# A first routing pass in the lead-out of attention, tables in pieces, and another order of passes and gathers

## What is computed

```
x = x + attention0(layernorm(x)); x = x + swiglu(layernorm(x)); x = x + attention1(layernorm(x))   # causal
z = layernorm(x)
for _ in range(2):                                   # LOOPS
    z_norm = rmsnorm(z) * norm_w
    scores = softmax(z_norm @ router_w)              # 8 experts
    vals, idx = top_k(scores, 2); vals = vals / (sum(vals) + 1e-9)
    mixed = sum over the two chosen e of  vals_e * ((silu(z_norm @ w1[e]) * (z_norm @ w3[e])) @ w2[e])
    z = z + mixed
x = x + z
```

## Time and profile before

| | us |
|---|---|
| median of three runs (2305.61 to 2311.1) | 2308.6 |
| the profiled execution, its own time | 2307.91 |
| its span, first to last instruction | 2306.2 |
| mean granted clock of TensorE | 0.959 of full |
| the attention's last addition to x (L902) ends | 1550.6 |
| first tile's transpose on PE | 1600.0 |
| last issue of the last gather | 2294.4 |

### The profile page before, as it was taken

The page is one execution under the profiler, slowest core; times in us unless marked ns, Lnnn a source line. Parts: engine busy times, 40 slices in busy tenths (PEclk is TensorE's granted clock), DMA queues, the critical chain, the costliest instruction groups (busy, mean ns, idle before and its releaser), DMA issues. The chain is left out here.

```text
span 2306.2 us, 47356 instructions
## 1 busy us (share of the span) xinstructions
PE 2011.8 (87%) x14679; PEld 982.9 (43%) x14679; DVE 1844.3 (80%) x5277; ACT 1462.1 (63%) x3354; POOL 1232.1 (53%) x1710
## 2 busy tenths in 40 slices
PE   5999999999988999899999999974888988988991
PEld 1222222222222465444444444432555766766661
DVE  8999999999999576888888888847777676676555
ACT  1788888888888332677777777751545655655550
POOL 6343343343321021676767676634476777667776
PEclk9999999999999999899999999985999999999996
DMA  7355344344341001434232433302233443433453
GB/s 183 102 130 139 102 130 139 102 129 139 102 129 48 1 19 37 100 70 101 69 99 71 96 74 93 76 26 74 87 106 101 122 117 114 118 108 113 130 139 99
DMA packets 224610, 226.94 MB, mean 98 GB/s; under 512 B 34032, under 2 KB 187504, under 8 KB 224368
## 3 DMA queue, kind: packets, MB, share of 16 engines
q1 hardware_dynamic: 152432, 164.62, 27.0%
q0 software_dynamic: 16384, 33.59, 5.0%
q10 hardware_dynamic: 55552, 25.71, 3.9%
HBM read 96.48 MB, written 125.76 MB: 96 GB/s over the span
## 5 line engine op out<-in xcount | busy, mean ns | idle before, releaser
L702 ACT ACTIVATE mid_PT<-mid_ps 128x512 f32<-128x512 f32 (+2 forms) x1792 | 914.0, 568 | 258.4 <-PE mid_ps L583 250.5
L785 DVE TENSOR_REDUCE mid_nmax<-mid_ps 128x1 f32<-128x512 f32 (+2 forms) x1280 | 776.4, 657 | 61.5 <-PE mid_ps L562 36.4
L562 PE MATMUL mid_ps<-KT,QT 48*128 48x512 bf16 (+3 forms) x2048 | 604.5, 351 | 68.3 <-DVE mid_nmax L785 49.6
L583 PE MATMUL mid_ps<-QT,KT 64*128 64x512 bf16 (+3 forms) x2048 | 562.5, 346 | 2.5 <-ACT mid_PT L702 2.2
L599 PE MATMUL mid_ps<-mid_PT,vv 128*32 128x512 f32 (+3 forms) x4096 | 465.1, 527 | 16.3 <-POOL mid_PT L914 12.5
L562 PEld LDWEIGHTS mid_ps<-KT,QT 48*128 48x128 bf16 x2048 | 158.9, 94 | 585.2 <-DVE mid_nmax L785 397.4
L782 DVE CUSTOM_DVE_ANT_0 mid_PT<-mid_ps,mask 128x512 bf16<-128x512 f32 (+1 forms) x512 | 304.5, 619 | 68.8 <-PE mid_ps L562 64.0
L1395 PE MATMUL moe_ps<-moe_w,moe_xinT 128*128 x638 | 341.5, 618 | 0.0
L1506 POOL DMA_INDIRECT rows_in<-moe_xn,moe_scat_idx x256 | 250.2, 977 | 161.9 <-DVE moe_scat_idx L1696 86.0
L1519 POOL DMA_INDIRECT moe_yg<-rows_out,moe_gat_idx x256 | 250.8, 980 | 80.6 <-issue 77.2
L1450 ACT ACTIVATE moe_xinT<-moe_ps,norm_w 128x128 f32<-128x128 f32 x319 | 116.7, 366 | 275.8 <-PE moe_ps L1407 186.9
(11 more groups left out here) (266 smaller groups left out, 3060.0 us busy)
## 6 DMA issues: line engine op xcount, KB each, us to landing
l_spread<-mid_slots SPq DMA_DIRECT2D x128, 384.0 KB, 5.4
rows_in<-mid_blank SPq DMA_DIRECT2D x64, 512.0 KB, 3.8
QT<-l_spread SPq DMA_DIRECT2D x128, 192.0 KB, 4.3
KT<-l_spread SPq DMA_DIRECT2D x128, 192.0 KB, 5.2
moe_xin<-rows_in SPq DMA_DIRECT2D x319, 64.0 KB
rows_out<-moe_y ACTq DMA_DIRECT2D x319, 64.0 KB
x<-in_L_attn_x_dram SPq DMA_DIRECT2D x8, 512.0 KB, 6.6
QT<-mid_mrows SPq DMA_DIRECT2D x256, 6.0 KB
```

Of the source, the lines that this page charges most:

```text
L562: mm = pe.matmul(ps[:, bank, n_keys * a:n_keys * (a + 1)], QT[rows, par, pair, i * P:(i + 1) * P], KT[rows, par, pair, 0:n_keys], start=Tr ...
L583: mm = pe.matmul(ps[:, bank, m * a:m * (a + 1)], KT[rows, own, pair, i * P:(i + 1) * P], QT[rows, own, pair, SEQ - m:SEQ], start=True, sto ...
L702: act.activation(weights_of(r, i, heads), ps[:, ring(S2, n - 2, k), 0:widths[i] * len(heads)], ACT.Exp, scale=scale).then_inc(exp_done, 1)
L785: dve.tensor_reduce(to, of, X_AXIS, ALU.max, negate=True).then_inc(s1_used, 1)
```

## The change

- Pass 0 moves into the lead-out of the causal attention (new class `Lead`): its norm on DVE to step 64, place 0; the transposes on PE to step 65, places 5 and 7, the router product to place 14; the choice on DVE to step 65, place 15; the count's nine matmuls and the row numbers to the end of step 66, the weights to the end of step 67. POOL issues the first 3 of the 16 DMAs of s0 at the end of step 67, the other 13 at the start of `experts`. Its working space lies in memory that the attention no longer uses.
- SP issues the ten weight loads at the end of the attention's block, after the last weighted values are made (`av_done`). The weights now lie in the buffer of the attention weights.
- Constants of `experts` are made earlier: two by POOL after its first step, others by DVE at step 64. POOL does one `iota` instead of three at the start of `experts`.
- `make_tables` is cut into up to 8 pieces, stages 20 to 27 of a pass, at the spacing of the pass's other stages. Unit 0's pieces run one after another before pass 1. SP waits for a new semaphore, `rows_made`, set by piece 5 (row numbers and experts), and no longer for the last piece.
- `begin` and `transfers` change.

Core of the diff (the body of `Lead` repeats the stages of pass 0 and is cut to its places and waits):

```diff
+class Lead:
+    ZT, SCRATCH, SENT = 14464, 15488, 3
...
+    def tensor(self, pe, off, u, s1_used, s1_total):
+        if (off, u) in ((1, 5), (1, 7)):
+            a = (u - 5) // 2
+            if a == 0:
+                pe.wait_ge(s1_used, s1_total)
+                pe.wait_ge(self.z_ready, 1)
+            for t in range(4):
+                mm = pe.transpose(self.psT[a][:, t * P:(t + 1) * P], self.z[:, 4 * a + t, :], self.w["ident"][:, :])
+            mm.then_inc(self.t_made, 1)
+        if (off, u) == (1, 14):
+            pe.wait_ge(self.t_used, 2)
+            for t in range(IT):
+                mm = pe.matmul(self.psR[:, t, :], self.zT[:, t * P:(t + 1) * P], self.w["router"][:, :], start=True, stop=True)
+            mm.then_inc(self.r_made, 1)
+        if (off, u) == (2, 15):
+            pe.wait_ge(self.const, 2)
+            pe.wait_ge(self.sel_ready, 1)
...
+    def scalar(self, act, off, u):
+        if (off, u) in ((1, 8), (1, 11)):
...
+        if (off, u) == (2, 8):
+            act.wait_ge(self.shifted, 1)
...
+            act.wait_ge(self.second_ready, 1)
...
+    def vector(self, dve, off, u, x_added):
+        if (off, u) == (0, 0):
...
+            dve.tensor_tensor(self.xn[:, :, :], self.z[:, :, :], each_row(rstd), ALU.mult).then_inc(self.xn_ready, 1)
+        if (off, u) == (1, 15):
+            c = self.linked
+            dve.wait_ge(self.r_made, 1)
...
+        if (off, u) == (2, 15):
+            c = self.linked
+            dve.wait_ge(self.k_made, 1)
...
+        if (off, u) == (3, 15):
+            c = self.linked
+            dve.wait_ge(self.exp_ready, 1)
...
+                if lead_pass and n == STEPS + 3:
+                    for i in range(lead_pass.SENT):
+                        lead_pass.scatter(pool, i)
...
             sp.wait_ge(zeroed, 16 * STEPS)
+            sp.wait_ge(second.signals["av_done"], STEPS)
+            load_experts(sp)
...
-    begin = {2: 0, 3: 14, 4: 29, 5: 47, 6: 63, 7: 78, 8: 95, 9: 115, 10: 135, 11: 157, 12: 179, 13: 201, 14: 223, 15: 246,
-             16: 270, 17: 283, 18: 292, 19: 314, 20: 325}
-    transfers = ("s0 s1 s2 s3 g8 s4 s5 g9 s6 g10 s7 g11 s8 g12 s9 g13 s10 g14 s11 s12 g15 s13 g16 s14 g17 g18 s15 "
+    begin = {2: 0, 3: 10, 4: 22, 5: 36, 6: 49, 7: 62, 8: 78, 9: 97, 10: 117, 11: 137, 12: 158, 13: 179, 14: 200, 15: 224,
+             16: 256, 17: 270, 18: 286, 19: 308, 20: 325}
+    transfers = ("s1 s2 s3 g8 s4 s5 s6 g9 s7 g10 s8 g11 s9 g12 s10 g13 s11 g14 s12 g15 s13 g16 s14 g17 s15 g18 "
                  "g19 g20 g21 g22 g23").split()
...
-        return [(k, s) for k, at in begin.items() for s in range(STAGES) if at + s * length(k) // STAGES == n]
+        return [(k, s) for k, at in begin.items() for s in range(STAGES + TABLES) if at + s * length(k) // STAGES == n]
...
-            for k in range(EARLY):
-                for s in range(STAGES):
+            for k in range(1, EARLY):
+                for s in range(STAGES + TABLES):
                     side(k, s)
...
                 if n == base_of[u]:
-                    sp.wait_ge(tables, u + 1)
+                    sp.wait_ge(rows_made, u + 1)
                     for k in range(first_of[u], first_of[u] + sizes[u]):
                         sp.wait_ge(scattered[k % 3], 16 * 2 * IT * (k // 3 + 1))
...
+            for i in range(lead.SENT, 2 * IT):
+                lead.scatter(pool, i)
...
-                    if k + 1 == first_of[unit_of[k]] + sizes[unit_of[k]]:
-                        make_tables(unit_of[k])
+                if s >= STAGES and k + 1 == first_of[unit_of[k]] + sizes[unit_of[k]]:
+                    make_tables(unit_of[k], s - STAGES)
...
+            for part in range(TABLES):
+                make_tables(0, part)
             run(tile, side, 0)
```

More of the change, by code:

```diff
@@ L1073, in middle @@
         after = After(one, ffn.signals)
-        second = attention(nc, ctx, "l1_", ps, shared, x, sides1, kept, center, causal=True, after=after)
+        second = attention(nc, ctx, "l1_", ps, shared, x, sides1, kept, center, causal=True, after=after, lead_pass=lead_pass)
         late = one["late"]
@@ L1180, in experts @@
     BANKS = 3
-    STAGES = 20
+    STAGES, TABLES = 20, 8
     sizes = [1] + [2] * (GROUPS - 1) + [1]
@@ L1705, in make_tables @@
                 full_u, passed_u, shares_u = full[:, :, 0:ht], passed[:, 0:n_tiles, :], shares[:, 0:n_tiles, :]
+                expert, before, live, row = (tab[:, a, 0:n_tiles] for a in range(4))
                 def per(t, n, k=P):
                     return t.unsqueeze(1).to_broadcast([k, n, EXPERTS])
[L1710 to L1712 removed]
@@ L1720, in make_tables @@
-                c.link(dve.tensor_tensor(shares_u, passed_u, per(ntiles[0:1, :], n_tiles, 1), ALU.mult))
-                expert, before, live, row = (tab[:, a, 0:n_tiles] for a in range(4))
-                dve.tensor_reduce(before, shares_u, X_AXIS, ALU.add)
-                c.link(dve.tensor_reduce(expert, passed_u, X_AXIS, ALU.add))
-                c.link(dve.tensor_tensor(before, iota_f[0:1, 0:n_tiles], before, ALU.subtract))
-                dve.tensor_scalar(before, before, float(P), None, ALU.mult)
@@ new lines, in make_tables @@
+                if part == 3:
+                    dve.tensor_reduce(before, shares_u, X_AXIS, ALU.add)
+                    c.link(dve.tensor_reduce(expert, passed_u, X_AXIS, ALU.add))
+                if part == 4:
+                    c.link(dve.tensor_tensor(before, iota_f[0:1, 0:n_tiles], before, ALU.subtract))
+                    dve.tensor_scalar(before, before, float(P), None, ALU.mult)
+                    dve.tensor_scalar(live, expert, EXPERTS - 0.5, None, ALU.is_lt)
+                    c.link(dve.tensor_scalar(row, expert, float(CAP), None, ALU.mult))
+                    c.link(dve.tensor_tensor(row, row, before, ALU.add))
@@ new lines, in make_tables @@
+                if part == 5:
+                    own = slice(base_of[u], base_of[u] + n_tiles)
+                    dve.tensor_tensor(row_of[0:1, own], row, live, ALU.mult)
+                    code = coded[:, :, :].rearrange("o c i -> o (c i)")[:, 0:n_tiles]
+                    c.link(dve.tensor_tensor(code, expert, live, ALU.mult))
+                    c.link(dve.tensor_tensor(weighted[:, 0:n_words, :], coded[:, 0:n_words, :], places[:, 0:n_words, :], ALU.mult))
+                    c.link(dve.tensor_reduce(sums[:, 0:n_words], weighted[:, 0:n_words, :], X_AXIS, ALU.add))
+                    dve.tensor_copy(words[0:1, word_of[u]:word_of[u + 1]], sums[:, 0:n_words]).then_inc(rows_made, 1)
+                    dve.wait_ge(rows_made, u + 1)
```

319 lines of the change are left out of this document (221 added, 98 removed).

## The result

| | median us | runs | lowest to highest |
|---|---|---|---|
| before | 2309.6 | 4 | 2305.6 to 2311.1 |
| changed | 2281.3 | 4 | 2274.6 to 2283.7 |

A forecast was written before the change was run, and what follows sets the result against it. POOL's queue of 31 transfer groups, 20.45 us each, was taken as the bound. Gains of 18.2 + 44.1 = 62.3 from 2307.9 gave 2245.6, with 0.7 for the median 2246; range 2232 to 2271, or 2275 if tiles set the end.

The forecast's parts named there:

- rival of longer issues: POOL's DMA issues: denser DVE work beside them makes each group 1 us longer, 2277 in all; chance 0.05.
- Part 1: Pass 0 moved into the attention's lead-out: 22.7 us removed, 4.5 added, net gain 18.2 us.
- I take 4.5, ends 1 and 8: Attention's end: PE's added transposes, router product and count matmuls delay it by 4.5 us, between 1 and 8.
- between 0 and 1 us: End of the attention's block: SP's ten weight loads end about with it and cost 0 to 1 us, taken as 0.
- DVE part hidden: Lead-out: DVE's first part of pass 0, about 12 us, fits into 15.05 us of idle time and costs nothing.
- Part 2: Expert loop: tables in pieces, earlier passes and a new queue order cut POOL's idle after s1 from 58.1 to 14 us.
- a first-loop pass adds 5.9: Tile times: each first-loop pass adds 5.9 us to its tiles' own 1.63 us each.
- 3.5 per table: Tile times: a table in pieces costs 3.5 us for units 1 to 3, against 7.8 for a whole table.
- I add 4: Row numbers of pass 2: pass 3's stages on DVE, in front of pass 2's last ones, delay them by 4 us.
- gain of 44.1 from pieces, beginnings and queue together: Expert loop: POOL's waits after s1 fall from 58.1 to 14 us, a gain of 44.1, ends 6 and 35.
- third rival: Expert loop: passes begin sooner and end no sooner, POOL's waits remain, only the lead-out's gain counts: 2290; chance 0.03.
- slower rival: Expert loop: 56 table pieces each hold up a tile, then PE runs at half clock; 1.7 us each, 2314; chance 0.02.

The follow-up runs named there:

- e3: Changed kernel with VectorE's z of pass 0 held until POOL's last masks are made: 2279.4 us, 0.9882 of before.
- c1: Changed kernel with only VectorE's first part of pass 0 (statistics, z, xn) in the lead-out, weights loaded in the experts' block; other, slower chip: 0.9942 of before.
- e7: Kernel before with only pass 0 moved into the lead-out; old beginnings, old transfers, whole tables; other, slower chip: 0.9951 of before.
- e1: Changed kernel with the ten weight loads back at the start of the experts' block: 2280.5 us, 0.9889 of before.
- e2: Changed kernel with all sixteen scatters of pass 0 issued in the experts' block, none in the lead-out: 2277.0 us, 0.9873 of before.
- r5: Changed kernel with the beginnings and transfers of before; pass 0 in the lead-out and tables in pieces stay: 2281.4 us, 0.9884 of before.
- r7: Kernel before with only pass 0 moved into the lead-out; old beginnings, old transfers, whole tables: 2300.2 us, 0.9967 of before.

## Why the prediction was wrong

- **What bounds the kernel: right.** POOL's queue of 31 groups, 20.48 us each against 20.45, and a tail of 11.0 against 10.9. The rival of longer issues fell.
- **Part 1, the term "I take 4.5, ends 1 and 8": wrong, 11.3.** The sum of products at the 1.2 GHz level, 6.4, was the upper end, and it is what they cost (2 x 1.11 + 3.58 + 0.56). I let PE's idle time absorb some and priced the attention's own products as before. In fact 1.6 us of idle time were added behind slow masks (2.75 in front of L794 against 1.19 before). The remaining 3.3 are a difference, not a measurement: they fit the attention's own work, which ran at 1.00 from 1536 to 1544 before and at 0.50 until 1552 now. e3 gives the masks 1.5; c1 against e7 gives the products and what goes with them 7.4 of 9.3.
- **Part 1, the block's end at "between 0 and 1 us": wrong, 4.1.** I asked what stands behind the ten loads on SP, and not what the three scatters wait for that share the DMA engines with them. e1 and e2 each remove the gap. "The three early issues gain nothing" was too kind: together with the loads they cost 4. In e2, without them, PE waits 0.95 us for the load of tile 0; in e1, with them, it does not.
- **"DVE part hidden": wrong by some 2 us.** DVE had the time for it, but POOL's masks beside it did not stay as they were. I had asked of POOL's DMA issues alone whether a busier DVE lengthens them, and for those the answer stands, 20.48 us against 20.45 per group. The Trainium skill (GPSIMD Engine Reference, Key points) says that GpSimd contends with DVE instructions that have two SBUF inputs. The trace of the masks agrees: 4.08 us against 2.40 beside two such instructions.
- **Tile 0 waits for pass 1 and not for rows: right,** with no wait for its load.
- **Part 2, "a first-loop pass adds 5.9" and "3.5 per table": the step that failed most.** Both are prices of passes that stand apart. On the old beginnings they nearly hold: r5 took 173.0 us for 80 tiles, and 130.6 for the tiles and 5.1 x 5.9 = 30 for the passes leave 12, some 4 to 5 per table. Laid back to back, 196.4 - 130.6 - 6 x 5.9 = 30 us are left for three tables, three times the forecast. 3.5 of it are the wait at tile 23, and PE waits some 10 us more for DVE than in r5. That this comes from stages of two passes in the same tiles is argued from DVE's timeline, and not shown by a run of its own.
- **"I add 4" for pass 3's stages in front of pass 2's last: right in kind.** s2 came 39.6 us after tile 0 instead of 33.9, so the term was nearer 9 than 4; with pass 3 at tile 14 (r5) it comes 33.0 after.
- **The gain of 44.1 from pieces, beginnings and queue together: wrong in its cause.** What was gained, 18.6, belongs to the pieces (18.8 from r7 to r5). I took a pass that begins sooner for one that ends sooner. The third rival ("passes begin sooner and end no sooner", 0.03) was right for the schedule, and wrong only in letting the pieces count for nothing.
- **The slower rival's mechanism did not come:** no wait on PE for y over 2.5 us, and the clock at 1.00 from 1788 to 2231 (0.93 in the 80 tiles before).
- **Slips in the sums, none of which changes the reading.** The low end, with 1 and 6 put in, is 2235 and not 2232. The products at full clock come to 3.5 and not 3.8. By its own terms s2 starts 34.2 us after tile 0 and not 33.9, s3 follows s2 with no idle time and not 2, and T at tile 75 leaves out the third table, 3.5.

## What to carry to other kernels

A schedule that starts work sooner is worth something only if the engine that does it has time there: price a stage by the stretches in which the new neighbours already lie beside it, and if there is none, take the price of what stands apart as the lower bound. Split the long task first, and measure that alone; here it was all the gain in the loop, and the new beginnings without it came out 32 us above the same kernel with it. Work put on a lead-out is not free because an engine is idle there: here it cost TensorE its time at the 1.2 GHz level, and POOL's masks were slower beside it.
